# GpSimd takes over the normalise of columns 108 to 512 and the residual add in the small FFN, and the self loops are taken out behind the FFN's second chunk

## The chip, the cores and the metric

The kernel runs on one core of one Trainium2 chip. The metric is the device time of one execution in microseconds (us), as the median of several runs. The core's engines are TensorE (PE in the profile, its weight loads PEld), VectorE (DVE), ScalarE (ACT), GpSimd (POOL) and the queue that issues transfers (SP). They run side by side, each in its own order, and wait for one another on semaphores.

## The reference, cut to what matters

Four layers work on x (1250 nodes, 512 columns, float32). Each adds its result to x, and each works on a layer norm of x:

```python
x = x + gnn0(layernorm(x), edges)     # three graph convolutions, with self loops
x = x + ffn0(layernorm(x))            # the small FFN, this document's place
x = x + gnn1(layernorm(x), edges)     # SAGE: mean over neighbours, two 512x512 products
x = x + ffn1(layernorm(x))            # mixture of 16 experts and a shared one
```

The layer norm takes mean and variance over the 512 columns of a row: (x - m) / sqrt(v + 1e-5). The small FFN decodes four nibbles from columns 16 to 80 of its input (the first of 16 columns above 0.5), takes columns 105 and 106 as two more features, and columns 0 to 2 as marks. It runs two networks of three small layers (160 wide) on these features for two positions of each node. The output is its whole input, the normalised x, with something added in columns 128 to 160 alone. So the residual is x + norm(x) in all 512 columns, and then small additions in 33 of them. The second graph layer uses the same edge list as the first, but without the self loops.

## The kernel before, in words

The 1250 nodes lie in ten tiles of 125 partitions (NT = 10, NP = 125). X holds x, XN the normalised x, each 512 columns a tile. CTR is the table of edge counts between nodes, 125 partitions by 10 tiles by 1250 columns. self_loops adds the identity to its ten diagonal blocks before the first graph layer, and subtracts it again (L1357) before the second graph layer, which waits for it on the semaphore minus_ready.

The order on each engine is written out by hand, with semaphores between the engines. Around the small FFN, VectorE does this:

- For the last of the three graph convolutions it adds each tile to X (L1445) and takes its statistics (L1447, L1448).
- deviations(1) makes the reciprocal deviations. Ten normalise instructions (recorded at L1223, the helper's line) write columns 0 to 108 of XN, the head that the features and marks need (IN1 = 108).
- The nibble features are made (L1458 to L1475, one write of feats per position and feature), and feat_ready lets TensorE transpose them in 20 pieces (L935). Then come the masks (L1479 to L1485): three compares and five products of ten columns.
- Ten more normalise instructions write columns 108 to 512 of XN.
- L1492 splits the transposed features into a high and a low part, in five pieces of 500 columns. ScalarE writes the high part first (L705). TensorE's first layer (L948) waits for these pieces.
- Then a loop over five chunks of 500 rows (c = 0 to 4, NRC = 5). For each chunk VectorE makes the low parts of the first hidden layer (L1499) and the second (L1507), adds XN to X for two tiles (L1518), and takes the statistics of the new X outside columns 128 to 161 (L1522, L1523). In round 3 it also splits a weight matrix (L1397). In round 4, the last, it takes the self loops out.
- After the loop it waits for y3_turned, TensorE's transposes of the outputs (L980), and makes the outputs from them (L1532 to L1557), the remaining statistics, and the layer norm of the second graph layer.

TensorE's loop runs first(c), second(c-1), third(c-2) and turn_back(c-3); second (L960) holds 21 of a round's products, and waits for VectorE's and ScalarE's parts of its inputs. GpSimd makes masks and low parts of the FFN's weights while the first graph network ends (L498 to L526), and then has nothing to do until the second graph layer is done. xn_ready counts the written tiles of XN, ten for each layer norm after the first.

Of the kernel before, what the change touches and what calls it, by code (L numbers as in the profile page):

```python
# [14 lines left out]
ALU = mybir.AluOpType  # L15
# [8 lines left out]
D = 512  # L24
E = 41250
NP = 125
NT = N // NP
# [31 lines left out]
IN1 = 108  # L59
# [4 lines left out]
NRC = ROWS // RC  # L64
# [17 lines left out]
def build(nc, a, out):  # L82
    ctx = ExitStack()
    with ctx:
        def sb(name, shape, dt=F32):
            return ctx.enter_context(nc.sbuf_tensor(name, shape, dt))

        def sem(name):
            return ctx.enter_context(nc.semaphore(name))
# [12 lines left out]
        def at(name, offset, shape, dt=F32):  # L102

            return nc.alloc_sbuf_tensor_at(name, shape, dt, offset=BASE + offset)
# [6 lines left out]
        X = at("X", R_X, [128, NT, D])  # L111
        XN = at("XN", R_XN, [128, NT, D])
# [87 lines left out]
        mv = sb("mv", [128, NT, 2])  # L200
        sd = sb("sd", [128, NT])
        rstd = sb("rstd", [128, NT])
# [16 lines left out]
        var_ready, sd_ready, xn_ready = sem("var_ready"), sem("sd_ready"), sem("xn_ready")  # L219
# [11 lines left out]
        val_ready, yh_ready = sem("val_ready"), sem("yh_ready")  # L231
        wh_ready, w_ready = sem("wh_ready"), sem("w_ready")
        xn_added = sem("xn_added")
        lin_ready = sem("lin_ready")
        lin_read = sem("lin_read")
        pre_ready = sem("pre_ready")
# [123 lines left out]
        def counting(eng, s):  # L360

            seen = [0]

            def link(ins):
                seen[0] += 1
                ins.then_inc(s, 1)
                eng.wait_ge(s, seen[0])
            link.seen = seen
            return link
# [104 lines left out]
        def _(pool):  # L474
# [40 lines left out]
            for row in (FK - 1, 2 * FK - 1, FK3 - 1):  # L515
# [8 lines left out]
            pool.tensor_tensor(w1s[0:FK3, :], w1x[0:FK3, 0:W1C], w1x[0:FK3, W1C:2 * W1C], ALU.add  # L524
                               ).then_inc(ffn_weights, 1)
            pool.tensor_tensor(w2l[0:GU + 1], w2f, f32(w2h[0:GU + 1]), ALU.subtract).then_inc(ffn_weights, 1)  # L526

            pool.wait_ge(hp_ready, FT * len(SPLITS))
            pool.iota(thr[:, :], pattern=[[BS, NT]], base=0, channel_multiplier=0,
# [683 lines left out]
        def _(dve):  # L1213
            v = nc.vector
            link = counting(dve, step)
# [6 lines left out]
            def normalise(t, c0=0, c1=D):  # L1222
                return v.tensor_scalar(XN[0:NP, t, c0:c1], X[0:NP, t, c0:c1], mv[0:NP, t, 0:1], rstd[0:NP, t:t + 1],  # L1223
                                       ALU.subtract, ALU.mult)
# [84 lines left out]
            with dve.If(slow > 0):  # L1309
# [6 lines left out]
                with dve.Fori(0, PASSES) as w:  # L1316
# [19 lines left out]
                    with dve.Fori(0, NSG) as g:  # L1336
                        for j in range(CPG):
                            v.tensor_scalar(s_lo[0:CHUNK, j, 0:NP], s_iota[0:CHUNK, 0:NP],
                                            lo[0:CHUNK, bass.ds(g * CPG + j, 1)], None, ALU.is_equal)
                            ins = v.tensor_scalar(s_ohk[0:CHUNK, j, :], s_iota[0:CHUNK, :],  # L1340
                                                  s_key[0:CHUNK, bass.ds(g * CPG + j, 1)], None, ALU.is_equal)
# [33 lines left out]
            for t in range(NT):  # L1375
                ins = v.bn_stats(stats[0:NP, t, 0, :], X[0:NP, t, :])
            link(ins)
            for t in range(NT):
                ins = v.bn_aggr(mv[0:NP, t, :], stats[0:NP, t, 0, :])
# [3 lines left out]
            for s, (c0, w) in enumerate(SPLITS):  # L1383
                dve.wait_ge(deg_ready, s + 1)
                ins = v.tensor_copy(invc[:, c0:c0 + w], PS[:, s, 0:w])
# [9 lines left out]
            def split_weight(k, raw):  # L1395
                dve.wait_ge(wh_ready, k + 1)
                v.tensor_tensor(WL[:, :, :], raw, f32(WH[:, :, :]), ALU.subtract).then_inc(w_ready, 1)  # L1397
# [21 lines left out]
            for l in range(LAYERS):  # L1419
# [9 lines left out]
                for t in range(NT + 1):  # L1429
                    m = l * NT + t  # L1430
                    if t < NT:
# [3 lines left out]
                        if l == LAYERS - 1 and t < 2:  # L1435
                            dve.wait_ge(val_ready, NT * LAYERS)
                        ins = v.scalar_tensor_tensor(out=tmp[0:NP, t % 2, :], in0=PS[0:NP, 6 + m % 2, :],
                                                     scalar=dis[0:NP, t:t + 1], in1=bias[0:NP, l, :],
                                                     op0=ALU.mult, op1=ALU.add)
# [3 lines left out]
                    if l == LAYERS - 1 and t < NT:  # L1443
# [4 lines left out]
                        ins = v.bn_aggr(mv[0:NP, t, :], stats[0:NP, t, 0, :])  # L1448
# [4 lines left out]
            deviations(1)  # L1453
            for t in range(NT):
                ins = normalise(t, 0, IN1)
            link(ins)
            nib = XN[0:NP, :, 16:80].rearrange("p t (g j) -> p t g j", j=16)
            link(v.tensor_scalar(fk[0:NP, :, :, :], nib, 0.5, None, ALU.is_gt))  # L1458
            wjb = wj[0:NP, :].rearrange("p (a j) -> p a j", a=1)
# [11 lines left out]
            for pos in range(POS):  # L1471
# [3 lines left out]
                ins = v.tensor_copy(to[:, :, :, 2:4], three_of(XN[0:NP, :, 105:107]))  # L1475
            ins.then_inc(feat_ready, 1)

            for c in range(3):
                ins = v.tensor_scalar(msk[0:NP, c, :], XN[0:NP, :, c], 0.5, None, ALU.is_gt)  # L1479
# [3 lines left out]
            link(v.tensor_tensor(msk[0:NP, 7, :], msk[0:NP, 4, :], msk[0:NP, 1, :], ALU.mult))  # L1483
            link(v.tensor_tensor(msk[0:NP, 5, :], msk[0:NP, 4, :], msk[0:NP, 7, :], ALU.subtract))
            link(v.tensor_tensor(msk[0:NP, 6, :], msk[0:NP, 3, :], msk[0:NP, 5, :], ALU.add))  # L1485
            for t in range(NT):
                normalise(t, IN1, D).then_inc(xn_ready, 1)
            dve.wait_ge(xn_ready, NT)
            for c in range(NRC):
                dve.wait_ge(ft_hi, c + 1)  # L1490
                part = ft[:, c * RC:(c + 1) * RC]
# [3 lines left out]
            def h1_copy(c):  # L1495
                for j in range(3):
                    dve.wait_ge(h1_hi, 3 * c + j + 1)
                    n = TILE1[j]
                    v.scalar_tensor_tensor(out=h1l[c % 2][0:n, j, :], in0=PS[0:n, j, 0:RC], scalar=0.0,  # L1499
                                           in1=f32(h1h[0:n, c % 2, j, :]), op0=ALU.max, op1=ALU.subtract  # L1500
                                           ).then_inc(h1_lo, 1)

            def h2_copy(c):
                for j in range(3):
                    dve.wait_ge(h2_hi, 3 * c + j + 1)
                    n = TILE[j]
                    v.scalar_tensor_tensor(out=h2l[c % 2][0:n, j, :], in0=PS[0:n, 3 + j, 0:RC], scalar=0.0,  # L1507
                                           in1=f32(h2h[0:n, c % 2, j, :]), op0=ALU.max, op1=ALU.subtract
                                           ).then_inc(h2_lo, 1)

            h1_copy(0)
            for c in range(NRC):
                if c + 1 < NRC:
                    h1_copy(c + 1)
                h2_copy(c)

                for t in (2 * c, 2 * c + 1):
                    ins = v.tensor_tensor(X[0:NP, t, :], X[0:NP, t, :], XN[0:NP, t, :], ALU.add)  # L1518
                link(ins)

                for t in (2 * c, 2 * c + 1):
                    v.bn_stats(stats[0:NP, t, 0, :], X[0:NP, t, 0:OUT0])  # L1522
                    v.bn_stats(stats[0:NP, t, 1, :], X[0:NP, t, OUT1:D])  # L1523
                if c == 3:
                    split_weight(3, WRAW[:, :, :])
                if c == NRC - 1:

                    self_loops(ALU.subtract, minus_ready)
            dve.wait_ge(y3_turned, NRC)
            for net in range(2):  # L1530
# [6 lines left out]
                for pos in range(POS):  # L1537
                    view = yv[0:NP, net, pos * NT:(pos + 1) * NT, :]
                    ins = v.tensor_tensor(view, view, m, ALU.mult)
# [20 lines left out]
            for t in range(NT):  # L1560
                ins = v.bn_stats(stats[0:NP, t, 2, :], X[0:NP, t, OUT0:OUT1])
            link(ins)
            for t in range(NT):
                ins = v.bn_aggr(mv[0:NP, t, :], stats[0:NP, t, :, :].rearrange("p a k -> p (a k)"))
# [41 lines left out]
            for n, (f, s) in enumerate(FS_SECOND):  # L1606
# [5 lines left out]
                ins = v.bn_stats(hst[:, f, s, :], ht[:, f, c0:c0 + w])  # L1612
# [8 lines left out]
            for t in range(NT):  # L1621
# [4 lines left out]
                ins = v.bn_aggr(mv[0:NP, t, :], stats[0:NP, t, 0, :])  # L1626
# [41 lines left out]
            for t in range(NT):  # L1668
                ins = v.tensor_tensor(cum[0:NP, t + 1, :], cum[0:NP, t, :], q[0:NP, t, :], ALU.add)
# [78 lines left out]
            for k in range(TOPK):  # L1748
# [3 lines left out]
            ins = v.tensor_tensor(ohb[0:NP, :, 1, :], ohb[0:NP, :, 1, :],  # L1752
                                  wsel[0:NP, :, :].rearrange("p k (t o) -> p (k t) o", o=1).to_broadcast(A3), ALU.mult)
# [109 lines left out]
```

## Time and profile before

| | |
|---|---|
| median of 3 runs | 980.22 us (977.76 to 981.02) |
| the profiled execution | 980.72 us, its span 979.0 us |
| busy, share of the span | TensorE 87%, VectorE 51%, ScalarE 24%, GpSimd 11% |
| mean granted clock of TensorE | 0.943 of full speed |
| the stretch of the small FFN | about 348 to 415 us of the span |

The span reaches from the first to the last instruction. A busy share is an average over stages with different limits, so the stage around the change has to be read by itself: in the chain of waits, which follows the work that ended last back from step to step, in the timeline, which gives each instruction with its start, duration, columns and what ended the engine's idle time before it, and in the windows view, which gives each engine's busy time in a stretch and the granted clock of TensorE (1.00 is 2.4 GHz, 0.50 is 1.2 GHz).

### The profile page before, as it was taken

Reading aid. Unit: us, or ns where it says so; the run is one execution under the profiler, and the core shown is the slowest. Engines: PE = TensorE matmul, PEld = TensorE weight load, DVE = VectorE, ACT = ScalarE, POOL = GpSimd, SP = SyncE. Lnnn points to the kernel's source line nnn. Section 1 sums busy time; section 2 is a strip of 40 time slices with the busy share of each in tenths; the row PEclk is TensorE's granted clock in tenths of the full one; section 3 lists DMA queues with packets and bytes.
Section 4 is the critical chain, followed back from the end, with each engine's and each line's share of the span. In section 5 each row is a group of like instructions: output and inputs, shape, how many; then the busy total and the mean of one; then the engine's idle time right before and its main releaser. Section 6 shows DMA issues by size and latency. Waiting matters only on the chain.

```text
span 979.0 us, 12310 instructions
## 1 busy us (share of the span) xinstructions
PE 856.4 (87%) x3638; PEld 575.3 (59%) x3639; DVE 495.8 (51%) x919; ACT 234.2 (24%) x483; POOL 106.0 (11%) x163
## 2 busy tenths in 40 slices
PE   4997799999999949579998697999889999899993
PEld 2554578788788726368887543544445555454551
DVE  7997671431431797990246857534323343434331
ACT  2554311421421024252112011101111121112111
POOL 2000000000000300000000010100132323232321
PEclk9999789999999968889999598999999999999997
DMA  4600000000000010001001120340197657945352
GB/s 138 157 1 1 1 1 1 1 1 1 1 0 1 28 45 1 1 1 44 1 3 49 74 95 0 125 186 22 51 335 215 192 140 228 326 100 122 64 145 32
DMA packets 32119, 71.64 MB, mean 73 GB/s; under 512 B 4124, under 2 KB 4374, under 8 KB 32074
## 3 DMA queue, kind: packets, MB, share of 16 engines
q1 hardware_dynamic: 25802, 56.36, 17.0%
q0 software_dynamic: 6272, 14.68, 7.4%
q8 instruction: 28, 0.46, 0.2%
q14 instruction: 17, 0.14, 0.0%
HBM read 96.85 MB, written 12.72 MB: 112 GB/s over the span
## 4 chain that ended last, share of the span: by engine, by line
PE 71%; DVE 11%; DMA 7%; ACT 5%; issue 4%; ACTq 1%; SPq 1%; DVEq 0%; POOL 0%; POOLq 0%
PE PS L891 19%; PE PS L1106 12%; PE PS L921 9%; DMA WB<-in_b 6%; PE PS L1139 6%; PE PS L825 5%; PE PS L1014 5%; PE PS L1094 4%; PE PS L1124 3%; PE PS L960 3%; ACT YF L767 1%; ACT CTR L620 1%; PE PS L1126 1%; PE PS L1116 1%; DVE XN L1223 1%
## 5 line engine op out<-in xcount | busy, mean ns | idle before, releaser
L891 PE MATMUL PS<-CTR,YH 125*128 125x500 f32 (+1 forms) x480 | 166.9, 363 | 3.8 <-DVE YL L1393 3.4
L891 PE MATMUL PS<-CTR,YL 125*128 125x500 f32 (+1 forms) x480 | 165.1, 359 | 0.0
L1106 PE MATMUL PS<-WB,YF 128*128 x448 | 151.7, 493 | 11.5 <-DMA WB<-in_b 9.0
L1106 PEld LDWEIGHTS PS<-WB,YF 128*128 128x128 f32 x448 | 85.0, 192 | 80.7 <-issue 29.4
L891 PEld LDWEIGHTS PS<-CTR,YH 125*128 125x128 f32 x480 | 92.0, 192 | 22.4 <-DVE YL L1393 9.8
L891 PEld LDWEIGHTS PS<-CTR,YL 125*128 125x128 f32 x480 | 92.5, 193 | 12.6
L1139 PE MATMUL PS<-WB,YF 128*128 x168 | 80.9, 619 | 13.2 <-ACT YF L767 12.7
L825 PE MATMUL PS<-ET 125*128 125x130 f16 x494 | 71.0, 291 | 12.4 <-DVE ET L1276 6.8
L767 ACT COPY YF<-PS 128x384 f32<-128x384 f32 (+1 forms) x38 | 18.2, 478 | 221.7 <-PE PS L1116 221.7
L1426 DVE TENSOR_TENSOR ZL<-PS,ZH 128x500 fp32r<-128x500 f32 (+1 forms) x36 | 21.1, 591 | 93.0 <-ACT ZH L670 93.0
L825 PEld LDWEIGHTS PS<-ET 125*128 125x128 f16 x494 | 40.3, 116 | 43.8 <-ACT CTR L620 23.5
L1139 PEld LDWEIGHTS PS<-WB,YF 128*128 128x128 f32 x168 | 30.3, 193 | 47.4 <-issue 47.4
L1693 DVE TENSOR_TENSOR YF<-PS,WB 128x768 f32<-128x768 f32 x14 | 13.4, 958 | 84.8 <-PE PS L1106 84.8
L1094 PE MATMUL PS<-SW,XTF 128*125 128x384 f32 x160 | 54.0, 492 | 0.0
L575 POOL DMA_INDIRECT out<-YF,dest_i x28 | 44.9, 1603 | 83.6 <-ACT YF L786 77.0
L620 ACT CAST CTR<-PS 125x120 f32 x165 | 43.8, 265 | 33.8 <-PE PS L825 25.3
L1693 DVE TENSOR_TENSOR bias<-PS,WB 128x768 f32<-128x768 f32 x14 | 13.4, 958 | 73.5 <-PE PS L1106 73.5
L1276 DVE TENSOR_TENSOR ET<-ET 125x1950 f16<-125x1950 f16 x33 | 49.7, 1506 | 0.0
L921 PE MATMUL PS<-WH,ZH 128*125 128x512 f32 x120 | 47.3, 394 | 0.0
L921 PE MATMUL PS<-WL,ZH 128*125 128x512 f32 x120 | 47.3, 394 | 0.0
L921 PE MATMUL PS<-WH,ZL 128*125 128x512 f32 x120 | 47.2, 394 | 0.0
L670 ACT CAST ZH<-PS 128x500 fp32r<-128x500 f32 (+1 forms) x36 | 18.3, 508 | 110.8 <-PE PS L891 110.8
(327 smaller groups left out, 1228.2 us busy)
## 6 DMA issues: line engine op xcount, KB each, us to landing
WB<-in_w SPq DMA_DIRECT2D x28, 1536.0 KB
WB<-in_w SPq DMA_DIRECT2D x28, 768.0 KB
WB<-in_b SPq DMA_DIRECT2D x28, 384.0 KB
X<-in_x SPq DMA_DIRECT2D x1, 2500.0 KB
xn_dram<-XN SPq DMA_DIRECT2D x1, 2500.0 KB
out<-X SPq DMA_DIRECT2D x10, 250.0 KB
WNEXT<-in_W SPq DMA_DIRECT2D x2, 1024.0 KB, 15.5
SW<-in_w SPq DMA_DIRECT2D x1, 1536.0 KB, 6.6
```

Source lines behind the costliest of these rows:

```text
L575: pool.indirect_dma_start(out[:, :], bass.IndirectOffsetOnAxis(dest_i[:, k:k + 1], 0), yo[:, k, :], None, compute_op=ALU.add).then_inc(sca ...
L620: nc.scalar.copy(CTR[0:NP, :, bass.ds(places[g % LOADS], WIN)], PS[0:NP, g % 6, 0:KEYS].rearrange("p (t w) -> p t w", t=NT)[:, :, 1:SLOTS] ...
L825: return nc.tensor.matmul(PS[0:128, g % 6, 0:KEYS], oh_lo[lb % RING][0:CHUNK, c // OWN % BATCH, :, c % OWN], oh_key[b % RING][0:CHUNK, g % ...
L891: mm = nc.tensor.matmul(dest, lhs, rhs, start=(t == 0 and h == 0), stop=(t == NT - 1 and h == 1))
L921: mm = nc.tensor.matmul(PS[0:NP, 6 + n % 2, :], z[:, f, t * NP:(t + 1) * NP], w[:, f, :], start=(f == 0 and h == 0), stop=(f == FT - 1 and ...
L960: mm = nc.tensor.matmul(PS[0:TILE[j], 3 + j, 0:RC], w[rows, k, cols], x, start=(k == tiles[0] and h == 0), stop=(k == 2 and h == 2))
L1014: mm = nc.tensor.matmul(PS[:, 4 + n % 4, 0:w], wt[:, f, fo * 128:(fo + 1) * 128], z[:, f, c0:c0 + w], start=(f == 0 and h == 0), stop=(f = ...
L1094: mm = nc.tensor.matmul(PS[0:NP, 2 * k + h, 0:INTER], xt[:, f, t * NP:(t + 1) * NP], SW[:, f * H2 + h * INTER:f * H2 + (h + 1) * INTER], s ...
L1106: mm = nc.tensor.matmul(PS[:, 2 * k + h, 0:INTER], xgt[:, k, f, :], WB[:, bass.ds(off + (f * H2 + h * INTER), INTER)], start=(f == 0), sto ...
L1124: nc.tensor.matmul(PS[0:NP, 6 + k, :], tt[:, k, j, 0:NP], SW[:, O_W2 + j * D:O_W2 + (j + 1) * D], start=(j == 0), stop=False)
L1139: mm = nc.tensor.matmul(PS[:, 6 + k, :], tt[:, k, j, :], WB[:, bass.ds(off + (O_W2 + j * D), D)], start=(j == 0), stop=(j == 2))
L1276: return v.tensor_tensor(oh_key[b % RING][0:CHUNK], iota_key[0:CHUNK].rearrange("p n (o x) -> p o n x", o=1).to_broadcast(dims), key16[0:C ...
```

## The change

GpSimd gets the ten normalise instructions of columns 108 to 512 and the ten residual adds of whole tiles. It starts when the head slices are written (a new semaphore, head_ready) and goes tile by tile: normalise tile t, then add tile t - 1. VectorE no longer does either. Instead it waits in each round of the loop until GpSimd has added the round's two tiles (x_added), ahead of the statistics. The self loops are taken out in the round c = 1 and not in the last round.

```diff
+        head_ready, x_added = sem("head_ready"), sem("x_added")
...
             pool.tensor_tensor(w2l[0:GU + 1], w2f, f32(w2h[0:GU + 1]), ALU.subtract).then_inc(ffn_weights, 1)
 
+            pool.wait_ge(head_ready, 1)
+            for t in range(NT):
+                pool.tensor_scalar(XN[0:NP, t, IN1:D], X[0:NP, t, IN1:D], mv[0:NP, t, 0:1], rstd[0:NP, t:t + 1],
+                                   ALU.subtract, ALU.mult).then_inc(xn_ready, 1)
+                if t:
+                    pool.wait_ge(xn_ready, t)
+                    pool.tensor_tensor(X[0:NP, t - 1, :], X[0:NP, t - 1, :], XN[0:NP, t - 1, :], ALU.add).then_inc(x_added, 1)
+            pool.wait_ge(xn_ready, NT)
+            pool.tensor_tensor(X[0:NP, NT - 1, :], X[0:NP, NT - 1, :], XN[0:NP, NT - 1, :], ALU.add).then_inc(x_added, 1)
+
             pool.wait_ge(hp_ready, FT * len(SPLITS))
...
                 ins = normalise(t, 0, IN1)
-            link(ins)
+            ins.then_inc(head_ready, 1)
+            dve.wait_ge(head_ready, 1)
...
-            for t in range(NT):
-                normalise(t, IN1, D).then_inc(xn_ready, 1)
-            dve.wait_ge(xn_ready, NT)
             for c in range(NRC):
                 dve.wait_ge(ft_hi, c + 1)
...
-                for t in (2 * c, 2 * c + 1):
-                    ins = v.tensor_tensor(X[0:NP, t, :], X[0:NP, t, :], XN[0:NP, t, :], ALU.add)
-                link(ins)
-
+                dve.wait_ge(x_added, 2 * c + 2)
                 for t in (2 * c, 2 * c + 1):
                     v.bn_stats(stats[0:NP, t, 0, :], X[0:NP, t, 0:OUT0])
                     v.bn_stats(stats[0:NP, t, 1, :], X[0:NP, t, OUT1:D])
                 if c == 3:
                     split_weight(3, WRAW[:, :, :])
-                if c == NRC - 1:
+                if c == 1:
 
                     self_loops(ALU.subtract, minus_ready)
```

## Rows read from the trace of the kernel before

**Rows 1.** The chain of waits, 345 to 364 us: start, length, step.

```profile
348.76 2.56 DVE XN L1223 x10
...
357.07 3.30 DVE XN L1223 x8
...
360.39 3.31 DVE FTT L1492 x5
```

**Rows 2.** The timeline, 351 to 361 us: start, length, engine, line, operation.

```profile
351.35 0.49 DVE L1458 TENSOR_SCALAR FS<-XN 125x640 f32<-125x640 f32 x1
351.88 0.83 DVE L1460 TENSOR_TENSOR FS<-FS,wj 125x640 f32<-125x640 f32 x1
352.74 0.82 DVE L1463 TENSOR_REDUCE FS<-FS 125x40 f32<-125x640 f32 x1
...
354.48 0.20 DVE L1473 COPY FS<-FS 125x30 f32<-125x30 f32 x1
...
355.02 0.32 DVE L1479 TENSOR_SCALAR msk<-XN 125x10 f32<-125x10 f32 x3
...
356.06 0.17 DVE L1485 TENSOR_TENSOR msk<-msk 125x10 f32<-125x10 f32 x1
...
356.27 4.09 DVE L1223 TENSOR_SCALAR XN<-X,mv,rstd 125x404 f32<-125x404 f32 x10
...
358.72 1.03 ACT L705 CAST FTT<-PS 15x500 fp32r<-15x500 f32 x2 [0.27 <-PE PS L935]
```

**Rows 3.** Windows: stretch, its length, busy PE, PEld, DVE, ACT, POOL, then PEclk.

```profile
366.20:372.00 5.80, 5.80 (x15) 4.23 (x15) 2.14 (x4) 1.71 (x4) 0.00 (x0) 0.50 0.00 0
380.00:402.00 22.00, 22.00 (x98) 14.04 (x97) 19.64 (x37) 11.84 (x20) 0.00 (x0) 1.00 0.01 1
```

**Rows 4.** The timeline at the end of the loop, 402 to 408 us.

```profile
402.58 1.28 DVE L1518 TENSOR_TENSOR X<-X,XN 125x512 f32<-125x512 f32 x2
...
404.89 1.32 PE L980 MATMUL PS<-ident,Y 8*125 8x8 f32 x8
...
405.15 2.06 DVE L1357 TENSOR_TENSOR CTR<-CTR,ident 125x125 fp32r<-125x125 f32 x10
...
407.14 0.18 DVE L1532 TENSOR_TENSOR FS<-PS,FFNR 125x40 f32<-125x40 f32 x1
```

**Rows 5.** The timeline inside the loop, behind the second chunk.

```profile
383.85 1.83 DVE L1499 SCALAR_TENSOR_TENSOR H1L<-PS,H1H 108x500 fp32r<-108x500 f32 x3
...
389.50 0.17 PEld L960 LDWEIGHTS PS<-H1H,W2H 108*107 108x107 f32 x1 [0.37 <-issue]
```

**Rows 6.** The timeline of VectorE and GpSimd, 328 to 334 us.

```profile
328.78 1.09 POOL L520 TENSOR_SCALAR W1X<-W1HI,FMASK 15x322 f32<-15x322 f32 x1
...
329.69 0.69 DVE L1445 SCALAR_TENSOR_TENSOR X<-tmp,X 125x512 f32<-125x512 f32 x1
329.84 0.61 POOL L522 TENSOR_TENSOR W3S<-FFNR,W3S 107x12 fp32r<-107x12 f32 x1
330.43 0.76 POOL L524 TENSOR_TENSOR W1S<-W1X 15x322 fp32r<-15x322 f32 x1
...
331.16 1.88 POOL L526 TENSOR_TENSOR W2L<-FFNR,W2H 108x960 fp32r<-108x960 f32 x1
...
332.49 1.10 DVE L1445 SCALAR_TENSOR_TENSOR X<-tmp,X 125x512 f32<-125x512 f32 x1
```

**Rows 7.** The timeline near the kernel's start, 6.5 to 7.5 us.

```profile
6.59 0.29 POOL L492 TENSOR_SCALAR_AFFINE_SELECT ident<-ident 128x128 f32<-128x128 f32 x1 [0.16 <-POOL cj L489]
6.65 0.42 DVE L1238 TENSOR_SCALAR ET<-ET 125x330 f32<-125x330 f32 x1
6.84 0.38 POOL L494 TENSOR_SCALAR_AFFINE_SELECT below<-below 128x128 f32<-128x128 f32 x1
7.10 0.33 DVE L1239 TENSOR_SCALAR ET<-ET 125x330 f32<-125x330 f32 x1
```

## The prediction

> **What bounds the kernel now.** I read the chain of waits first, over the stretch that the change touches. Between the first graph network and the small FFN's first weight products the steps are VectorE's: ten head slices normalised from 348.76 us (2.56 us), the nibble features, the masks, and from 356.27 us on the normalise of columns 108 to 512 [rows 1, 2]. Only then comes the second half of the feature split (L1492) at 360.39 us, which TensorE needs for its first product. So the 4.09 us that the ten wide normalises take in the timeline are on the path [rows 1, 2], apart from what ScalarE's copies (L705) would keep VectorE waiting anyway: the last two of them end at 358.72 + 1.03 = 359.75 us [rows 2].
>
> The windows view then shows TensorE without a gap, 22.00 of 22.00 us, from 380 to 402 us [rows 3]. Inside the FFN loop VectorE is no bound: whatever it loses or gains there is hidden. After the loop VectorE bounds again. Its last residual add starts at 402.58, the self loops run 405.15 to 407.21, and only at 407.14 does it turn to the FFN's outputs, while TensorE's last transposes of them had ended at 404.89 + 1.32 = 406.21 us [rows 4].
>
> **The change part by part.**
>
> *Normalise leaves VectorE.* If nothing else moved, the five L1492 instructions (3.31 us, 0.66 each) would be paced by ScalarE, and the last would start at about 359.8 and end at 360.45 instead of 360.39 + 3.31 = 363.70 us [rows 1, 2]: 3.2 us gained.
>
> *Residual adds leave the loop.* Two adds take 1.28 us [rows 4] in each of five rounds. Four of the five are hidden behind TensorE [rows 3] and are worth nothing. The fifth lies behind the last chunk.
>
> *Self loops move behind the second chunk.* There they take 2.06 us [rows 4], where 1.28 us of adds have gone, so this second round grows by 0.8 us and the split of the fourth chunk would start at about 384.7 in place of 383.85 and end 1.83 us later, at 386.5; TensorE's products on it start at 389.50 us [rows 5]. Three us of cover are left: cost nothing. If the cover were gone it would cost 0.8 us.
>
> *The end.* Without adds and self loops (1.28 + 2.06 = 3.3 us) VectorE would be ready at about 403.9 and wait for the transposes until 406.2: what is late next is TensorE's last third layer and ScalarE's copy. Start 406.25 in place of 407.14: 0.9 us gained.
>
> So the gains are 3.2 + 0.9 = 4.1 us.
>
> *What GpSimd now does, and what it disturbs.* GpSimd gets ten normalises of 404 columns and ten adds of 512 columns, back to back from 351.3 us, when the head slices are ready. Its rows in the trace: a scaling by one pointer of 322 columns took 1.09 us; two-tensor subtractions of 322 and 960 columns took 0.76 and 1.88 us [rows 6]. The partitions (15 or 108) I take to make no difference. By columns a normalise is 1.09 x 404 / 322 = 1.37 us. Between the two subtractions a column costs 1.76 ns, so an add is 0.76 + 190 x 1.76 ns = 1.09 us. The mean is 1.23 us, all twenty 24.6 us. They would end near 376 to 378 us. The first round's wait needs five instructions (6.3 us of work) and comes behind the second layer of the first chunk, on which TensorE is busy until 372 us and beyond even before any delay [rows 3]; the last needs all twenty and comes at 402.58 - 3.2 = 399.4 us [rows 4]. So the new waits on x_added cost nothing. GpSimd would become the bound only at 48 us / 20 = 2.4 us an instruction, twice the rows.
>
> The costly thing is the other one. The trace shows that GpSimd and VectorE instructions that both read SBUF shut each other out. VectorE's two-tensor L1445 takes 0.69 us; the one started at 332.49 took 1.10, and ended 0.55 us after GpSimd's L526 had ended at 333.04. A GpSimd subtraction of only 12 columns took 0.61 us because L1445 ran from 329.69 to 330.38 [rows 6]. It is not only two-tensor work: VectorE's L1238, one SBUF input, took 0.42 us while GpSimd's L492 ran to 6.88, against 0.33 for the same shape at 7.10, and GpSimd's L494 behind it took 0.38 against 0.29 [rows 7]. Both pairs also show the order: they take turns. Between two GpSimd instructions that stand back to back, one waiting VectorE instruction gets in, and then the next GpSimd one.
>
> The Trainium skill (SBUF — State Buffer, "SBUF: two separate sides") states that VectorE instructions in a two-port mode or with two SBUF inputs and GpSimd instructions lock the shared pair for a whole instruction. The trace agrees by 1.10 against 0.69 us and 0.42 against 0.33 us [rows 6, 7]. By the rule the sum is the one below; if engines shared without waiting it would be 4.1 us of gain.
>
> Now count what VectorE has to do from 351.35 us on. One-input work here runs nearly twice as fast as two-tensor work: 640 columns in 0.49 against 0.83 us [rows 2]. So the compare L1458, the small scalings and copies are of L1238's kind, the product L1460 and the mask products of L1445's. Ahead of the transposes stand L1458, L1460, L1465, L1466 and six copies; behind, three compares and five products for the masks: 18 instructions. L1458 starts level with GpSimd and I let it go first; 17 then meet a GpSimd instruction. The reduce L1463 reads one tensor at the slow rate (640 columns in 0.82 us) and the memset L1468 reads nothing: I let both run freely; were they to wait too, it would be 1 to 2 us more. L1492 and the later splits read PSUM and one SBUF tensor; at most one or two GpSimd instructions are left by then, so at most 1.2 us, and I take nothing.
>
> What one meeting costs: GpSimd's 1.23 us less the time between VectorE's instructions in which GpSimd runs anyway. Eight of the 17 stand behind a semaphore of their own, with about 0.20 us from start to start (L1485 at 356.06, the next at 356.27); nine follow at once, with 0.09 us, as the copies do (0.20 us each, six from 354.48 to 355.02) [rows 2]. So 8 x 1.03 + 9 x 1.14 = 18.5 us. Beside the reduce (0.82 us) and the memset (about 0.4 with its gap, an estimate) GpSimd works on without harm: less 1.2. VectorE reaches the end of the masks at 356.27 + 17.3 = 373.6 us, and L1492 then starts at 373.6 in place of 360.39: 13.2 us late. The transposes of the features come some 10 us late and are done before that. TensorE's clock is 0.50 of full speed (1.2 GHz) from 366.2 to 372.0 us, after sparse work, and full from about there [rows 3]; the sequence of work ahead of the rise is the same, only later, so I take no difference.
>
> Sum: 13.2 - 0.9 = 12.3 us later. The profiled execution is 980.72 us (span 979.0, with 1.7 around it), 0.5 above the median of the three runs, 980.22. So 980.2 + 12.3 = 992.5 us.
>
> The terms that the trace does not show: a normalise on GpSimd does two operations with two pointers, no row has that. Bound below: the select of 128 columns in 0.29 us [rows 7], by columns 0.92 us for 404; mean 1.0; 8 x 0.8 + 9 x 0.91 - 1.2 = 13.4, so 9.3 - 0.9 = 8.4 us later. Bound above: each operation costs the row's full time, 2.74 us; mean 1.9; 8 x 1.7 + 9 x 1.8 - 1.2 = 28.6, 24 us later. I take the row of the same instruction kind. The Trainium skill (GPSIMD Engine Reference, "Engine selection") calls one-input work on GpSimd roughly line rate, which by its clock is an estimate of 0.34 us a normalise and would make the sum 3.6 us later; the row of 1.09 us for 322 columns speaks against it [rows 6].
>
> **The rivals.**
>
> *Turns only at the semaphores.* If GpSimd can't get in between VectorE instructions that follow at once, only 8 meetings are left (L1460, L1465, L1466, the run of copies and compares, and four of the products): 8 x 1.03 - 1.2 = 7.0 us, L1492 at 363.3, 2.9 - 0.9 = 2 us later: 982.2, with 1 to 3 us more if some runs are split. For it: six copies in 0.54 us leave only slivers between them. Against: the small ones use the memory for a small part even of their 0.09 us, and a waiting GpSimd got in at once in rows 6 and 7.
>
> *No meeting matters, faster.* If small VectorE instructions slip through, the 4.1 us are gained: 976.1. It decides where a meeting costs less than about 0.3 us (17 x 0.3 = 5.1, less 1.2, is 3.9). Place: 351.3 to 356.3 us. Against it are the whole-instruction waits of rows 6 and 7; for it, that no row shows an instruction of 10 to 60 columns.
>
> *Normalise cheaper than its nearest row.* 8.4 us later by the bound, 988.6; the skill's figure, were it to hold, gives 983.8.
>
> *GpSimd is too slow for the loop.* At over 2.4 us an instruction the adds are late too: over 1000.
>
> **Chances.** Turns at every instruction, +10 to +17: 0.52, likeliest. Cheaper normalise, or turns at part of the runs, +5 to +10: 0.14. Turns at semaphores only, +1 to +5: 0.16, of which 0.07 under 0.3% (2.9 us, about what a measurement can tell). Gain: 0.13, of which 0.01 under 0.3%. Dearer GpSimd, over +17: 0.05. So faster 0.12, same 0.08, slower 0.80. The range 982 to 1000 us leaves out the gain and the smallest losses below and the dearest GpSimd above, near 0.2.
>
> **What would show it.** In the profile after: L1460, L1465, L1466, the copies L1473 to L1475 and the mask products with durations of 1.0 to 1.5 us, each ending with or just after a GpSimd row; the feature transposes near 365 in place of 355.17 us; L1492 near 373.6 us; the GpSimd group from 351.4 to about 377 us; self loops in the second round with no idle TensorE; the last net's start 0.9 us nearer to the end of the loop. I am wrong if VectorE's small instructions keep their 0.16 to 0.20 us beside GpSimd, or if GpSimd's rows are far from 1.23 us.

## The result, and the profile after

The changed kernel took 974.18 us (median of 11 runs, 969.87 to 978.68), the kernel before 977.76 us beside it (11 runs, 975.15 to 981.02). The ratio is 0.9954, with a 95% interval of 0.9932 to 0.9976: 4.5 us faster, by the interval 2.3 to 6.6. Forecast were 992.5 us and 982 to 1000. The forecast was wrong in sign; its rival "no meeting matters", with 976.1 us, came nearest in the number. Its reason, that small VectorE instructions slip through, is not what the runs show (e3 below).

The span of the profiled execution fell from 979.0 to 969.5 us. The timeline of the changed kernel from the head slices to the masks (start, length, engine, line; code lines are 6 to 12 higher here, L1472 is L1460 of before, L1485 to L1487 are the copies L1473 to L1475):

```profile
349.17 2.55 DVE L1234 TENSOR_SCALAR XN<-X,mv,rstd 125x108 f32<-125x108 f32 x10
351.75 0.49 DVE L1470 TENSOR_SCALAR FS<-XN 125x640 f32<-125x640 f32 x1
351.83 3.72 POOL L531 TENSOR_SCALAR XN<-X,mv,rstd 125x404 f32<-125x404 f32 x2 [18.40 <-DVE XN L1234]
352.28 1.18 DVE L1472 TENSOR_TENSOR FS<-FS,wj 125x640 f32<-125x640 f32 x1
353.50 0.82 DVE L1475 TENSOR_REDUCE FS<-FS 125x40 f32<-125x640 f32 x1
354.35 0.19 DVE L1477 TENSOR_SCALAR FS<-FS 125x40 f32<-125x40 f32 x1
354.57 0.20 DVE L1478 SCALAR_TENSOR_TENSOR FS<-FS 125x40 f32<-125x40 f32 x1
...
355.25 0.35 DVE L1485 COPY FS<-FS 125x30 f32<-125x30 f32 x1
...
355.52 1.31 DVE L1485 COPY FS<-FS 125x30 f32<-125x30 f32 x1
355.52 1.25 POOL L535 TENSOR_TENSOR X<-X,XN 125x512 f32<-125x512 f32 x1
356.73 0.19 DVE L1486 COPY FS<-FS 125x30 f32<-125x30 f32 x1
356.77 1.74 POOL L531 TENSOR_SCALAR XN<-X,mv,rstd 125x404 f32<-125x404 f32 x1
...
356.93 0.72 DVE L1491 TENSOR_SCALAR msk<-XN 125x10 f32<-125x10 f32 x3
357.07 4.35 PE L946 MATMUL PS<-ident,FS 125*15 125x125 f32 x20 [11.10 <-DVE FS L1487]
...
358.80 3.98 DVE L1501 SCALAR_TENSOR_TENSOR FTT<-PS,FMASK,FTT 15x500 fp32r<-15x500 f32 x5 [0.26 <-ACT FTT L716]
```

Hold this against [rows 2]. The two-tensor product takes 1.18 in place of 0.83 us, one copy 1.31 in place of 0.2, the three compares 0.72 in place of 0.32. But L1477 and L1478, in the middle of a normalise, take 0.19 and 0.20 us: they didn't wait. Only the copy that met the residual add L535 was shut out for the add's whole length, and ended just behind it (356.83 against 356.77). Seventeen whole-instruction waits were forecast; there is one.

The chain of waits shows what sets the loop's start now: TensorE's own transposes of the features, then ScalarE's copy, then VectorE's last split (start, length, step).

```profile
357.07 4.36 PE PS L946 x20
361.46 0.57 ACT FTT L716
362.03 0.02 issue
362.05 0.73 DVE FTT L1501
362.78 0.66 DVE H1L L1508
```

The groups of GpSimd's instructions, 350 to 383 us (busy time, mean ns of one):

```profile
L531 POOL TENSOR_SCALAR XN<-X,mv,rstd 125x404 f32<-125x404 f32 x10 | 17.4, 1738 | 18.4 <-DVE XN L1234 18.4
L535 POOL TENSOR_TENSOR X<-X,XN 125x512 f32<-125x512 f32 x9 | 11.4, 1270 | 0.0
```

The windows view (columns as in [rows 3]) and four lines of the timeline, where TensorE's products become fast, at the self loops and at the end of the loop:

```profile
366.20:372.00 5.80, 5.80 (x20) 4.12 (x18) 1.96 (x4) 1.17 (x2) 5.80 (x5) 0.70 0.00 0
```

```profile
369.63 0.44 PE L971 MATMUL PS<-H1H,W2L 106*107 106x500 f32 x1
...
380.64 2.92 DVE L1368 TENSOR_TENSOR CTR<-CTR,ident 125x125 fp32r<-125x125 f32 x10
...
403.27 1.32 PE L991 MATMUL PS<-ident,Y 8*125 8x8 f32 x8
...
404.63 0.20 DVE L1538 TENSOR_TENSOR FS<-PS,FFNR 125x40 f32<-125x40 f32 x1 [2.34 <-PE PS L991]
```

VectorE now waits 2.34 us for the output transposes, where it came 0.9 us late in [rows 4].

The prefix ahead of this place varies by execution: the nibble compare started at 351.16 to 351.37 us in the four executions without GpSimd's new work and at 351.25 to 352.82 us in the nine with it. No run says why, and the table leaves it out. So I count from the start of the nibble compare, "the start" from here on (351.35 us before, 351.75 in the changed kernel). Each number is read from the timeline of that run's profiled execution; "Products fast" is the start of the first of the second layer's products that takes under 0.5 us, "output part" the start of the first instruction that reads the transposed outputs (L1532 of before), and the last column is the end of the span less the start of the next full-width normalise.

| run | transposes start | feature splits end | products fast | output part | from layer norm to the end |
|---|---|---|---|---|---|
| before | 3.82 | 12.35 | 20.80 | 55.79 | 563.6 |
| e10, before again | 3.82 | 12.36 | 20.38 | 55.55 | 559.8 |
| e11, before a third time | 3.83 | 12.37 | 19.98 | 55.42 | 565.7 |
| changed | 5.32 | 11.03 | 17.88 | 52.88 | 556.5 |
| e8, changed again | 5.32 | 11.03 | 17.87 | 52.91 | 556.5 |
| e1, normalises first | 4.60 | 10.02 | 18.04 | 52.32 | 557.9 |
| e2, start behind the features | 3.82 | 9.42 | 17.86 | 55.34 | 559.9 |
| e3, twelve more adds | 8.20 | 16.65 | 23.43 | 59.00 | 562.1 |
| e4, self loops alone | 3.83 | 12.36 | 19.98 | 54.66 | 559.2 |
| e5, normalise alone | 4.60 | 10.01 | 18.02 | 53.17 | 559.0 |
| e6, behind features, loops third | 3.82 | 9.53 | 15.17 | 50.58 | 559.4 |
| e7, self loops last | 5.32 | 11.02 | 17.87 | 52.88 | 560.1 |
| e9, six more scalings | 4.87 | 10.25 | 18.25 | 52.53 | 562.9 |

The middle columns repeat closely from run to run, the last varies by 5.9 us for one and the same kernel (559.8 to 565.7). So the gain of the region is 55.79 - 52.88 = 2.9 us, against the mean of the three profiles of before (55.59) 2.7. It consists of 1.3 us (splits, 12.35 to 11.03), 0.7 us (the products become fast 2.9 us earlier, 1.6 of it ahead of what the splits alone bring, so fewer of them run at the slow clock) and 0.9 us (VectorE no longer late at the end): the output transposes end at 52.84 in place of 54.86 us, and the output part follows after 0.04 in place of 0.93 us. The 0.7 us are a count, not a cause shown: e2 and e6 run the same code up to there, with the same front, and their products became fast at 17.86 and 15.17 us.

### The profile page after: what moved, and what is told of

Read it like the earlier page. It is cut to its first block, busy times and chain, and to the rows that moved or that the text cites. A ratio compares the mean times of both kernels' runs of the same rounds, so it can differ in the third digit from the quotient of the medians.

```text
span 969.5 us, 12310 instructions
## 1 busy us (share of the span) xinstructions
PE 852.5 (88%) x3638; PEld 572.0 (59%) x3639; DVE 488.8 (50%) x899; ACT 233.8 (24%) x483; POOL 134.7 (14%) x183
## 3 DMA queue, kind: packets, MB, share of 16 engines
q1 hardware_dynamic: 25802, 56.36, 17.3%
## 4 chain that ended last, share of the span: by engine, by line
PE 74%; DVE 10%; DMA 6%; ACT 5%; issue 4%; ACTq 1%; SPq 0%; DVEq 0%; POOL 0%; POOLq 0%
PE PS L902 19%; PE PS L1117 13%; PE PS L932 9%; PE PS L1150 6%; PE PS L836 5%; PE PS L1025 5%; DMA WB<-in_b 5%; PE PS L1105 4%; PE PS L1135 3%; PE PS L971 3%; ACT YF L778 2%; ACT CTR L631 1%; PE PS L1127 1%; PE PS L1137 1%; PE PS L1067 1%
## 5 line engine op out<-in xcount | busy, mean ns | idle before, releaser
L1117 PE MATMUL PS<-WB,YF 128*128 x448 | 150.4, 489 | 7.8 <-DMA WB<-in_b 5.3
L1150 PE MATMUL PS<-WB,YF 128*128 x168 | 79.4, 609 | 13.2 <-ACT YF L778 12.7
```

What stands on the lines that cost most here:

```text
L1117: mm = nc.tensor.matmul(PS[:, 2 * k + h, 0:INTER], xgt[:, k, f, :], WB[:, bass.ds(off + (f * H2 + h * INTER), INTER)], start=(f == 0), sto ...
L1150: mm = nc.tensor.matmul(PS[:, 6 + k, :], tt[:, k, j, :], WB[:, bass.ds(off + (O_W2 + j * D), D)], start=(j == 0), stop=(j == 2))
```

## The experiments

**Normalises first (e1).** Which GpSimd instruction shuts VectorE out?

```diff
             for t in range(NT):
                 pool.tensor_scalar(XN[0:NP, t, IN1:D], ...).then_inc(xn_ready, 1)
-                if t:
-                    pool.wait_ge(xn_ready, t)
-                    pool.tensor_tensor(X[0:NP, t - 1, :], ...).then_inc(x_added, 1)
-            pool.wait_ge(xn_ready, NT)
-            pool.tensor_tensor(X[0:NP, NT - 1, :], ...).then_inc(x_added, 1)
+            for t in range(NT):
+                pool.wait_ge(xn_ready, t + 1)
+                pool.tensor_tensor(X[0:NP, t, :], ...).then_inc(x_added, 1)
```

> GpSimd does all ten normalises and then all ten adds, so beside VectorE's features and masks it runs normalises alone. Read: from the end of the ten head slices to the start of TensorE's feature transposes (L946 there), 5.32 us in the changed kernel (351.75 to 357.07), 3.82 us before (351.35 to 355.17). Theory 1 (the prediction's: every VectorE instruction that needs the second port waits for a whole GpSimd instruction): with 1.70 us a normalise the stretch grows to over 15 us. Theory 2 (a two-tensor GpSimd instruction shuts VectorE out for its whole length, a normalise only for about 0.55 us from its start): the 1.1 us that one copy lost to the first add goes, at most three starts of 0.2 to 0.4 us remain, so 4.2 to 4.8 us. Theory 3 (it depends on VectorE's instruction alone, small ones seldom wait): about 5.3 us as in the changed kernel, one small one still loses about 1 us. Total by theory 2: 0.5 to 1 us faster than the changed kernel, no difference by theory 3.

The stretch was 4.60 us, as theory 2 says, the splits ended at 10.02 us. One run: 972.83 us, against 981.18 for one run of the kernel before beside it. In its timeline the normalises stand back to back over the whole stretch, and VectorE lost time at three places: at L1470 (1.18 against 0.83 us), at the copies from 356.03 on (0.15), and at the last copy:

```profile
352.61 17.35 POOL L531 TENSOR_SCALAR XN<-X,mv,rstd 125x404 f32<-125x404 f32 x10 [18.40 <-DVE XN L1232]
353.06 1.18 DVE L1470 TENSOR_TENSOR FS<-FS,wj 125x640 f32<-125x640 f32 x1
...
355.13 0.19 DVE L1475 TENSOR_SCALAR FS<-FS 125x40 f32<-125x40 f32 x1
355.36 0.20 DVE L1476 SCALAR_TENSOR_TENSOR FS<-FS 125x40 f32<-125x40 f32 x1
...
356.47 0.60 DVE L1485 COPY FS<-XN 125x60 f32<-125x60 f32 x1
```

VectorE's features and masks ran beside the first three normalises. No delay reaches the 1.70 us of a normalise; the largest is 0.41 us. Behind the second chunk the ten self loops took 3.53 us in place of 2.06, for they met GpSimd's last two adds.

**Twelve more adds (e3).** The reverse: beside the features and masks GpSimd runs two-tensor adds alone. They write a scratch tile that nothing reads; the rest of the computation stays whole.

```diff
             pool.wait_ge(head_ready, 1)
+            for k in range(12):
+                if k >= 2:
+                    pool.wait_ge(extra, k - 1)
+                pool.tensor_tensor(tmp[0:NP, k % 2, :], X[0:NP, k % NT, :], X[0:NP, k % NT, :], ALU.add).then_inc(extra, 1)
```

> GpSimd first does twelve additional two-tensor adds of 512 columns (X + X into a scratch tile that nothing reads), then its work as in the changed kernel. Beside the features and masks it thus runs two-tensor instructions of 1.27 us alone. Theory 1 and theory 2 agree here, and tell the term that the prediction got right or wrong: every linked VectorE instruction with two inputs or at double rate waits for a whole add, L1472, L1477, L1478 and at least one copy before the transposes: 4 x 1.07, the stretch is at least 8 us; if GpSimd also gets in between the unlinked copies (six and more meetings) it is 13 to 15 us. Theory 3 (small ones seldom wait): 5.5 to 7 us. The total is 12 to 20 us slower than the changed kernel by theory 1 or 2, since the real work starts 15 us late as well.

```profile
351.30 13.00 POOL L534 TENSOR_TENSOR tmp<-X 125x512 f32<-125x512 f32 x12 [18.37 <-DVE XN L1239]
351.78 1.54 DVE L1477 TENSOR_TENSOR FS<-FS,wj 125x640 f32<-125x640 f32 x1
353.36 0.82 DVE L1480 TENSOR_REDUCE FS<-FS 125x40 f32<-125x640 f32 x1
354.21 1.04 DVE L1482 TENSOR_SCALAR FS<-FS 125x40 f32<-125x40 f32 x1
355.29 0.98 DVE L1483 SCALAR_TENSOR_TENSOR FS<-FS 125x40 f32<-125x40 f32 x1
356.40 0.31 DVE L1485 MEMSET FS<- 125x300 f32 x1
356.74 0.52 DVE L1490 COPY FS<-FS 125x30 f32<-125x30 f32 x1
357.16 0.18 DVE L1491 COPY FS<-FS 125x30 f32<-125x30 f32 x1
357.25 1.04 DVE L1492 COPY FS<-XN 125x60 f32<-125x60 f32 x1
358.19 0.18 DVE L1490 COPY FS<-FS 125x30 f32<-125x30 f32 x1
358.28 1.03 DVE L1491 COPY FS<-FS 125x30 f32<-125x30 f32 x1
```

This is the picture that the forecast had drawn for the change. The same 40-column instructions that passed a normalise in 0.19 and 0.20 us take 1.04 and 0.98 us, and five of the eight mask instructions of 10 columns 0.89 to 1.01 us; the reduce and the memset pass. Between copies that follow at once GpSimd gets in at every second one. So the stretch was 8.20 us, at the lower end (13 to 15 was for every one), and the splits ended at 16.65. That the total would be 12 to 20 us slower than the changed kernel was too much: the output part came 6.1 us later (one run: 982.49 us).

**Six more scalings (e9).** Is it the pointers or the kind of instruction? Scratch writes again:

```diff
+            for k in range(6):
+                if k >= 2:
+                    pool.wait_ge(extra, k - 1)
+                pool.tensor_scalar(tmp[0:NP, k % 2, :], X[0:NP, k % NT, :], 1.0, 2.0, ALU.subtract, ALU.mult).then_inc(extra, 1)
```

> GpSimd first does six additional scalings of 512 columns by two constants (one SBUF input, the normalise's two operations, no pointers), then its work as in the changed kernel. Why does a normalise shut VectorE out for only some 0.4 us of its 1.70? Theory 2a, the kind of instruction: a scaling takes 1.70 x 512 / 404 = 2.15 us and leaves VectorE alone after its start, so the stretch from the nibble compare to the transposes is 4.6 to 5.3 us. Theory 2b, the two pointers: without them a scaling takes under 0.8 us and holds for its whole length, as two-tensor adds do, so L1472 takes 1.2 us or more, L1477 and L1478 some 0.5, and the stretch is 6 to 9 us.

```profile
352.82 11.68 POOL L534 TENSOR_SCALAR tmp<-X 125x512 f32<-125x512 f32 x6 [18.38 <-DVE XN L1239]
353.29 1.11 DVE L1477 TENSOR_TENSOR FS<-FS,wj 125x640 f32<-125x640 f32 x1
...
355.29 0.38 DVE L1482 TENSOR_SCALAR FS<-FS 125x40 f32<-125x40 f32 x1
355.70 0.20 DVE L1483 SCALAR_TENSOR_TENSOR FS<-FS 125x40 f32<-125x40 f32 x1
...
356.37 0.62 DVE L1490 COPY FS<-FS 125x30 f32<-125x30 f32 x1
```

Without pointers a scaling took 11.68 / 6 = 1.95 us for 512 columns and delayed VectorE by 0.2 to 0.43 us at a time, the most at the copy of 356.37 us (0.62 against 0.19); the stretch was 4.87 us. Theory 2a: it is the kind of instruction. Whether the number of its inputs or its operation makes the kind, no run tells.

**Start behind the features (e2).**

```diff
-            pool.wait_ge(head_ready, 1)
+            pool.wait_ge(feat_ready, 2)
```

> GpSimd starts when the features are written (feat_ready at 2) and not when the head slices are, everything else as in the changed kernel. Read: the stretch from the end of the head slices to the transposes, and the end of the last L1501-type split of features, and the start of the output part (404.63 us in the changed kernel with TensorE's last first-network product ending 0.4 us later than before). All theories: the stretch is back at 3.8 us. Theory 1: the masks' eight instructions meet eight GpSimd instructions of 1.5 us and the feature splits start some 8 us late. Theory 2: one or two delays of under 1.3 us in the masks, hidden behind ScalarE's copies, so the splits end 1.9 us earlier than in the changed kernel (1.5 from the transposes and up to 0.4 from the masks), the output part starts about 2 us earlier, GpSimd ends near 386 us with no wait for it. Total 2 us faster than the changed kernel.

The front came out as expected: 3.82 us, splits' end at 9.42. Yet the output part was at 55.34 us, 2.5 us later than in the changed kernel. The timeline names the cause:

```profile
379.54 1.29 POOL L535 TENSOR_TENSOR X<-X,XN 125x512 f32<-125x512 f32 x1
379.61 6.57 DVE L1368 TENSOR_TENSOR CTR<-CTR,ident 125x125 fp32r<-125x125 f32 x10
...
382.51 1.28 POOL L535 TENSOR_TENSOR X<-X,XN 125x512 f32<-125x512 f32 x1
383.75 1.28 POOL L537 TENSOR_TENSOR X<-X,XN 125x512 f32<-125x512 f32 x1
...
386.91 1.55 PE L959 MATMUL PS<-FTT,W1S 15*108 15x500 f32 x3 [0.76 <-DVE H1L L1508]
...
390.46 0.62 PE L971 MATMUL PS<-H1H,W2L 108*107 108x500 f32 x1
```

The ten self-loop instructions behind the second chunk met GpSimd's last adds and took 6.57 us in place of 2.06. The split of the fourth chunk behind them was late and TensorE waited. All theories had missed that. Two of the ten lost nearly all of it (narrow windows of the same timeline):

```profile
379.61 2.03 DVE L1368 TENSOR_TENSOR CTR<-CTR,ident 125x125 fp32r<-125x125 f32 x1
```

```profile
382.15 3.03 DVE L1368 TENSOR_TENSOR CTR<-CTR,ident 125x125 fp32r<-125x125 f32 x1
```

The second of them began ahead of the last two adds and ended behind both, at 385.18 us: here VectorE got no turn between two adds, as it had in e3.

Up to the self loops e2 was 0.9 us ahead of the changed kernel. The self loops then cost 3.3 us: TensorE came 1.8 us late to the fourth chunk's second layer, and from about 390.1 to 393.5 us its products took 0.62 us again (granted clock 0.50 of full speed from 390.20 to 393.40), 1.5 us more. Ahead of this fall TensorE had waited for VectorE twice, which it does not in e6.

**Behind the features, self loops third (e6)** checks this: e2 with one more edit.

```diff
-                if c == 1:
+                if c == 2:
```

> GpSimd starts behind the features, and the self loops are taken out behind the third chunk, when GpSimd is done (near 34 us in; the third chunk's statistics end near 37). Theory 2: transposes at 3.8, splits' end at 9.4 us, self loops at 2.06 us for the ten in place of 6.57 us with the same start behind the second chunk, output part at 51.3 to 52.3 us. 3.5 to 4.5 us faster than before, 0.5 to 1.5 faster than the changed kernel. If the self loops were not what cost the 2.5 us in the run with the start behind the features, the output part stays near 55 us.

```profile
386.56 2.07 DVE L1368 TENSOR_TENSOR CTR<-CTR,ident 125x125 fp32r<-125x125 f32 x10
...
403.40 0.20 DVE L1538 TENSOR_TENSOR FS<-PS,FFNR 125x40 f32<-125x40 f32 x1 [2.34 <-PE PS L991]
```

The self loops are back at 2.07 us, the output part at 50.58 us, 5.2 us before that of the kernel before and 0.7 earlier than expected, since the products became fast at 15.17 us. The code up to there is that of e2, where they became fast at 17.86 us, and by the start of the third chunk's first layer e6 is 1.4 us ahead of e2. So of the 2.3 us below, 0.9 come with the front and 1.4 from where the clock rose in this one execution. The ratio to before is 0.9935 (0.9905 to 0.9965). It is the best by this region, 2.3 us ahead of the changed kernel; in total times it can't be told from it (below, 0.9942).

**One part alone: self loops (e4), normalise (e5), and the change with the self loops last (e7).** e4 is the kernel before with `if c == 1` at the self loops. e5 gives GpSimd the normalises, leaves the adds with VectorE in its loop (behind a wait on xn_ready) and the self loops last. e7 is the changed kernel with `if c == NRC - 1`.

> The kernel before with the self loops moved behind the second chunk, and nothing else. Read: the start of the output part behind TensorE's last output transposes. Before, VectorE came 0.9 us late to it (407.14 against 406.21 us). All theories: the gap closes to under 0.1 us, VectorE waits, 0.9 us gained; the second round's self loops cost nothing. If the change's 3 to 4 us came mostly from this part, the output part would start 3 us earlier relative to the first product of the first layer.

> One part alone: GpSimd does the ten normalises from the end of the head slices, VectorE keeps the residual adds in its loop, and the self loops stay behind the last chunk. Times from here on are counted from the start of the nibble compare (351.35 us before, 351.75 in the changed kernel, 352.53 with the normalises first). Theory 2: the transposes start at 4.6 us and the feature splits end at 10.0 us, as with the normalises first (3.8 and 12.35 before). GpSimd is done some 17 us in, before VectorE's first add, so the adds cost what they did. The output part starts 0.9 us behind the transposes, as before; at 52.5 to 53.5 us in place of 55.8. 2.3 to 3.3 us faster than before. By the prediction's theory (whole instructions, 1.70 us each) it would be over 15 us slower.

> The changed kernel with the self loops back behind the last chunk. VectorE's last statistics ended 2.3 us before the output transposes were done in the changed kernel, the self loops take 2.06 us, so they just fit: output part within 0.1 us of the transposes' end, at 52.9 to 53.0 us, and the total is that of the changed kernel. So moving the self loops would be worth nothing once the adds are gone, and the change's gain is all in the normalise and the adds. The rival, the prediction's sum, in which the 0.9 us needs both: the same time here would refute that only for the self loops.

e4: the output transposes end at 405.79, VectorE starts at 405.82 us: the 0.9 us are gained. The fast products began 0.8 us earlier than in the first profile of before, but no earlier than in its third (19.98). One run: 975.07 us. e5: splits' end at 10.01, GpSimd done after 17.35 us, the output part at 53.17 with VectorE 0.9 us late; 0.9975 (0.9941 to 1.0009), inconclusive in total. e7: the ten self loops ran 401.75 to 403.82 us in the shadow of the transposes:

```profile
401.75 2.07 DVE L1368 TENSOR_TENSOR CTR<-CTR,ident 125x125 fp32r<-125x125 f32 x10
...
404.17 0.20 DVE L1538 TENSOR_TENSOR FS<-PS,FFNR 125x40 f32<-125x40 f32 x1 [0.35 <-PE PS L991]
```

The output part is at 52.88 us as in the changed kernel, the ratio 0.9959 (0.9929 to 0.9989). Taking out the adds or moving the self loops is each enough for the 0.9 us at the end; together they bring no more.

**The same kernels again (e8, e10, e11).** No edit.

> The changed kernel itself beside the others, on the same chip, for comparing them: 3 to 5 us faster than before. The stretch from the nibble compare to the layer norm's first 512 column normalise was 64.09 us before and 61.21 after; if the rest of the 9.5 us between the two profiled executions was chance, it is 2.9 us again here, and behind the layer norm the time lies anywhere from 556 to 564 us, as it did in the six profiled executions so far.

> The kernel before itself, for a second profile. The first two profiled executions differ by 9.5 us in span, of which 2.5 us lie up to the layer norm behind the FFN and 7.0 behind it (563.6 before, 556.5 in the changed kernel and 556.5 again in its second profile; 558 to 563 us in the others). If the time behind the layer norm is chance from execution to execution, it lies anywhere between 556 and 564 us here. If the change itself shortened it, it is 563 again. From the nibble compare to the output part it is 55.8 us again, within 0.1.

> The kernel before a third time, with the same reading and the same two expectations: by chance anywhere between 556 and 564 us behind the layer norm, by an effect of the change 563 a third time; 55.8 us from the nibble compare to the output part.

e8: ratio 0.9942 (0.9911 to 0.9974). The region repeats to 0.03 us in the changed kernel and to 0.4 us in the kernel before (55.42 to 55.79, a little beyond the 0.1 that I expected). Behind the layer norm the kernel before took 559.8 and 565.7 us, so 563.6 was neither a fixed value nor the top. By the result's interval (at most 6.6 us in all, 2.7 of them in the region) no more than 3.9 of the 7.0 us can be the change's, and the rest is chance from execution to execution. That the changed kernel had 556.5 twice, below every other run, I can't explain; two profiles don't tell an effect from luck.

## Why the prediction was wrong

**The step that failed** is "What one meeting costs: GpSimd's 1.23 us less the time between VectorE's instructions", taken for each of 17 meetings. It held each GpSimd instruction to shut VectorE out for its whole length. For two-tensor adds that is right: e3 shows 1.04 and 0.98 us for instructions of 0.18 and 0.20. For a normalise it is wrong: e1 shows them in a row with no delay above 0.41 us, though one lasts 1.70. In the changed kernel the stretch held two normalises and one add, and VectorE's way to the transposes grew by 1.5 us (3.82 to 5.32): 0.35 at the product, 0.15 at the first copies, 1.1 less some overlap at the copy that met the add. Behind it the masks lost 0.4. The forecast had 17.3. The evidence for whole instructions, [rows 6] and [rows 7], was a two-tensor instruction of 1.88 us and a select of 0.29 us; the normalise was neither. The same rows held a weak hint that I passed over: L520, a scaling, ran to 329.87 us, and L1445, begun at 329.69 beside its end, took its plain 0.69 us.

The Trainium skill (SBUF — State Buffer, "SBUF: two separate sides") states a lock for the whole instruction for any GpSimd instruction. It fits the adds (1.04 against 0.18 us) and not the scalings (1.70 us long, 0.5 lost at most in any run). The measurement decides.

Where in a scaling VectorE waits, the timelines show, by each instruction's duration less its plain one. One that began 0.08 to 0.32 us into a scaling ran only from 0.46 to 0.57 us into it: the last feature copy in e1 (0.60 against 0.19 us), L1493 in e2 (0.54 against 0.17), a self loop in e9 (0.77 against 0.28, the largest loss). One that began 0.51 to 1.3 us into it took its plain time. Copies that began 1.35 us or more into it ended 0.05 us or more behind its end (in the changed kernel 0.35 us, in e9 0.62), while mask products of ten columns begun 1.40 to 1.71 us into it took 0.17 us. The first scaling of a run is apart: it began beside the compare, lasted 2.02 us, and the product beside it lost 0.35 us. Why the end holds copies and not these products, no run isolates.

The forecast's turns, one VectorE instruction between two GpSimd ones, hold in e3 and not everywhere: a self-loop instruction waited behind two adds in e2 (3.03 us), and in e1 one took 1.74 us, through the rest of one add and the whole next.

**Sizes.** The normalise took 1.70 to 1.74 us and not 1.37, the add 1.27 and not 1.09. Both were too small; it didn't matter, since x_added was never waited for: VectorE's waits in this stretch name ScalarE and TensorE alone. GpSimd ended at 381.62 in place of about 377 us. The one-input figure that the Trainium skill's GPSIMD Engine Reference ("Engine selection") gives, roughly line rate, is far from 1.70 us for 404 columns, as its row had said.

**The gain in front** was set at 3.2 us and measured 1.3 in the changed kernel. With the transposes unhindered (e2) it is 12.35 - 9.42 = 2.9 us, so the sum for this part was right to 0.3. It had ScalarE's copies pace the splits; what it missed is that these follow the transposes, which wait for feat_ready. So the 1.5 us lost ahead of the transposes are lost in full, and the 0.4 us at the masks, which came off VectorE's slack, cost nothing. The forecast let the transposes come late at no cost, because its masks came later still.

**The end**, 0.9 us, was right (0.93 to 0.04 us), though I ascribed it to the adds and the self loops together, and e4 and e7 show that either alone does it.

**The self loops** "cost nothing" came true in total, on a cover of 3 us. But 2.06 us became 2.92 by meeting the last add, the very contention that I had counted everywhere else; e2 shows that with GpSimd's end some 3.5 us later they cost 3.3 us.

**The clock.** Before, the granted clock stands at 0.50 of full speed (1.2 GHz) from 366.2 to 372.0 us [rows 3], and products take 0.62 us until one of 0.44 at 372.15. In the changed kernel the same window has 0.70 and the rise lies at 369.63. Ahead of it TensorE had done its transposes from 357.07 to 361.42 and products from 361.35 on, without the pause of about 2 us that before had between the two. I had taken no difference; it was 0.7 us, a quarter of the region's gain. In the kernel before, the rise itself lay at 19.98 to 20.80 us behind the start in three executions, in the changed kernel at 17.88 and 17.87 us in two. That it was the missing pause that moved the rise is not shown: e2 and e6 differ by 2.7 us there with the same code ahead of it.

**What the profile of the changed kernel should have shown**, by the forecast: durations of 1.0 to 1.5 us on some ten of VectorE's small instructions (two were there, the product, which is not a small one, and one copy), transposes near 365 (357.07), L1492's successor near 373.6 (358.80), GpSimd's group to 377 (381.62), and the output start nearer (it was).

**Of the 4.5 us** in total, the region explains 2.7 to 2.9, inside the interval of 2.3 to 6.6. The rest is not settled.

## What to carry to other kernels

Whether work on GpSimd disturbs VectorE depends on which GpSimd instruction stands beside which of VectorE's: put two-tensor GpSimd work beside VectorE work that reads PSUM or does reductions and statistics, not beside two-tensor work on SBUF or small copies and scalings. A GpSimd scaling can stand beside them more cheaply: it cost no VectorE instruction more than 0.5 us here. Place such work by when it ends as well as by when it starts: in e2 a better start pushed GpSimd's end into the self loops and lost more (3.3 us) than it had won (0.9). And before a contention seen on one kind of instruction is multiplied by seventeen, look for a row of the very kind, even one that shows no delay.

## What the runs showed of the hardware

- A GpSimd two-tensor add of 512 columns held VectorE's 40-column instruction for 1.04 us (0.18 alone), and between VectorE copies that follow at once it got in at every second one (1.04, 0.18, 1.03 us). A self-loop instruction in e2 had no such turn and waited behind two adds (3.03 us against 0.28).
- A GpSimd scaling of 404 columns lasted 1.70 us. VectorE instructions begun in its first third of a microsecond ran from 0.46 to 0.57 us into it (0.2 to 0.5 us lost), those begun 0.51 to 1.3 us into it lost nothing, and copies begun near its end waited for the end (0.15 us lost). Without pointers, 512 columns took 1.95 us with the same pattern, 0.43 us lost at the end.
- The add of X and XN took 1.27 us, that of X with itself 1.12 us on average with VectorE's turns inside.
- One kernel's time behind the layer norm varied from 559.8 to 565.7 us between executions, more than the change was worth.
